# One product split into three one-pass products, and one scan per sequence instead of one per pair

## The chip, the cores and the metric

The kernel runs on one core of one Trainium2 chip. The metric is device time in microseconds, from start to end of one execution. Three runs of the kernel before gave 936.23, 934.80 and 934.54 us, median 934.8 us. The profiled execution took 936.22 us.

## What is computed

The reference is a stack of two layers, each with an attention-like part and a feed-forward part, on x of shape (16, 256, 128), every part followed by a layer norm and a residual. Four parts follow one another:

- L0 attention: a long complex convolution along the sequence. With phazor = r·exp(i·theta) per channel the kernel computes it as a linear recurrence, y[t] = r·y[t-1] + u[t], on the cosine and the sine part of x, and then multiplies back.
- L0 FFN: eight small experts, two picked per token, and a shared expert.
- L1 attention: 16 heads, null keys, ALiBi, causal.
- L1 FFN: four experts, two picked per token. The second one (named `me` in the kernel) is

```
eq  = x @ me_eq_w + me_eq_b
sym = (eq @ me_wv + me_bv) @ me_wo + me_bo
e1  = gelu(sym @ me_c1w + me_c1b) @ me_c2w + me_c2b
```

The three linear maps before `me_c1w` and `me_c1w` itself are folded on chip into one 128x256 weight, `w_me`, so that the expert is `gelu(x @ w_me + b_me) @ w_c2`. The "first product" of the second expert is x @ w_me.

## The kernel before

**Tiling.** The 16 sequences are worked on in 8 groups of SEQ = 2 sequences, that is N = 512 tokens as T = 4 tiles of 128. A group passes through four stages, named by the first letter of their steps: `e` (convolution), `l` (L0 FFN), `a` (L1 attention), `f` (L1 FFN). In the steady state one pass of the tables holds `f` of group i-1, `a` of group i, `l` of group i+1 and `e` of group i+2.

**Order.** Nothing is scheduled on the fly. For every engine (PE, DVE, ACT, POOL) there are tables of step names, lines 36 to 185: PROLOGUE, FIRST, MIDDLE (played five times), LAST_L, LAST_A, LAST_F. An engine runs its steps in the order of its table and waits on semaphores inside them. All loads and stores of the steady state are issued by SP.

**Steps that the change and the prediction touch.**

- `s_decay` (L1298 to L1303, DVE, once): fills `decay_row` with r per channel, 512 columns, and sets columns 0 and 256 to zero, so that one scan over 512 columns restarts at the second sequence.
- `e_scan` (L1432 to L1443, DVE, once per group): two products of the transposed input with the cosine and sine tables (L1438), then two scans of 512 columns (L1443). Both scan operands lie in SBUF. The tensor_tensor_scan is `state = decay*state + u`.
- `s_gain2` (L1308, DVE, first group only) and `conv_gains` (L921, POOL): multiply the scans' outputs by the filter. In all groups `conv_gains` waits for the count of `l_conv`.
- `s_fold3` (L1836 on PE, L1104 on ACT): the folded weight is written to PSUM bank 2 and copied to `w_me`. `s_split` (L1372 to L1375, DVE) waits for that copy and signals `all_set`.
- `f_me.0` and `f_me.1` (L2133 to L2143 on PE, L1224 on ACT): for each half of the 256 hidden rows one fp32 matmul with 128 rows of weights and 512 columns, on `xm_full`, the float32 copy of the transposed, normalised tokens. ACT takes the gelu of each.
- `mm3` (L1761 to L1765, PE): a product of split operands. Every operand is kept as `hi`, rounded to fp32r, and `lo`, the rest, also fp32r. Three fp32r matmuls accumulate hi·hi, hi·lo and lo·hi. It is what `f_sw`, `f_ml`, `a_m`, `a_k`, `a_v`, `l_g` and `l_u` already use. The split tokens `xm` of the L1 FFN are made by ACT (`xm.hi`, L1212) and by DVE (`xm.lo`, `f_lows`, L1645, which counts `f_low`).
- `mask` (L944 to L959, POOL): for each attention unit two selects in place (L949) and one sum of two SBUF tensors (L959). DVE's `e_scan` stands between `a_mix.1` and `a_mix.2` in MIDDLE and POOL's selects run beside it.

In MIDDLE `f_me.0` follows `f_sw.0`, and `f_me.1` follows `f_ce2` and precedes `a_v.0`. In LAST_L it is `f_me.0` after `a_k.2`, `f_me.1` between `f_ml.1` and `f_ml.2`; in LAST_A `f_me.0` after `f_sw.1`, `f_me.1` after `f_sw.2`. In LAST_F, the last group alone, `f_me.0 f_me.1` come right after `f_ce.1` and before `f_sw.0`.

Of the kernel before, what the change touches and what calls it, by code (L numbers as in the profile page):

```python
# [18 lines left out]
F32 = mybir.dt.float32  # L19
# [3 lines left out]
ALU = mybir.AluOpType  # L23
ACT = mybir.ActivationFunctionType
AX_X = mybir.AxisListType.X

P = 128
# [201 lines left out]
def program(nc, a, out):  # L229
    x = a["L0_attn_x"]  # L230
    B, L, D = x.shape
    SEQ = 2
    G = B // SEQ
    T = SEQ * L // P
    N = T * P
# [9 lines left out]
    start = 2.0 ** (-2.0 ** (-1.0))  # L245
# [7 lines left out]
    with ExitStack() as ctx:  # L253
        def sb(name, shape, dt=F32):
            return ctx.enter_context(nc.sbuf_tensor(name, shape, dt))

        def sem(name):
            return ctx.enter_context(nc.semaphore(name))

        def signal(name, per):  # L260
            return Signal(sem(name), per)

        bank = [ctx.enter_context(nc.psum_tensor(f"bank{i}", [P, 512], F32)) for i in range(8)]
# [10 lines left out]
        def split_weight(name, width):  # L274
            return Split(sb(name + "_hi", [P, width], F32R)[:], sb(name + "_lo", [P, width], F32R)[:])
# [14 lines left out]
        conv_a = sb("conv_a", [P, L])  # L290
        conv_b = sb("conv_b", [P, L])
        conv_c = sb("conv_c", [P, L])
        decay_row = sb("decay_row", [P, N])
        vec = sb("vec", [P, 40])
        slope = sb("slope", [P, H])
        bias_k0 = sb("bias_k0", [P, H])
# [17 lines left out]
        w_sw1 = split_weight("w_sw1", I1)  # L314
        w_sw3 = split_weight("w_sw3", I1)
        w_sw2 = sb("w_sw2", [P, J1, P])
        w_me = sb("w_me", [P, 2 * P])
        w_c2 = sb("w_c2", [P, 2, P])
        w_f1 = sb("w_f1", [P, 2 * P])
        w_f2 = sb("w_f2", [P, 2, P])  # L320
# [22 lines left out]
        xm = xlT  # L343
        conv = sb("conv", [P, 4, N])
# [74 lines left out]
        col = {n: vec[:, i:i + 1] for i, n in enumerate(vlist)}  # L419
# [27 lines left out]
        time = kT[:, 0, 0:L + 1]  # L447
# [46 lines left out]
        f_scaled = sem("f_scaled")  # L494
        f_rounded = sem("f_rounded")
        f_split = sem("f_split")
        colb_made = sem("colb_made")
        nk_summed = sem("nk_summed")
        nk_rooted = sem("nk_rooted")
# [32 lines left out]
        def use(kind, t=0, k=0):  # L532

            return ring.index((kind, t, k))
# [3 lines left out]
        l_conv = signal("l_conv", 6)  # L538
# [49 lines left out]
        f_low = signal("f_low", 2)  # L588
# [6 lines left out]
        f_me = signal("f_me", 2)  # L595
# [49 lines left out]
        def ending(g):  # L645
            return g == G - 1
# [4 lines left out]
        def me_bank(g, j):  # L651
            return bank[2 + j] if ending(g) else bank[7]
# [13 lines left out]
        def xm_full(g):  # L666
            return xin[:].rearrange("p t d -> p (t d)") if ending(g) else conv[:, 2, :]
# [16 lines left out]
        def half(h):  # L684
            return slice(2 * h * P, 2 * h * P + 2 * P)
# [36 lines left out]
        def first(g):  # L722
            return known(g) and g == 0
# [272 lines left out]
        def _(act):  # L996
            n = [0]

            def made_by(i):
                n[0] += 1  # L1000
                i.then_inc(act_made, 1)
# [99 lines left out]

            def s_fold3():
                act.wait_ge(pe_made, 8)
                made_by(act.activation(w_me[:], bank[2][:, 0:256], ACT.Copy))  # L1104
                assert n[0] == ACT_MADE

            def to_cols(g):
# [148 lines left out]
        def _(dve):  # L1256
            n = [0]

            def link(i):

                n[0] += 1
                i.then_inc(made, 1)
                dve.wait_ge(made, n[0])
# [5 lines left out]
            V = nc.vector  # L1269
# [28 lines left out]
            def s_decay():  # L1298
                dve.wait_ge(act_made, 2)
                dve.wait_ge(pool_made, POOL_TIME)  # L1300
                dr = decay_row[:].rearrange("p (s t) -> p s t", s=SEQ)
                link(V.tensor_scalar(dr, time[:, 0:L].unsqueeze(1).to_broadcast([P, SEQ, L]), 0.0, col["r"], ALU.mult, ALU.add))
                link(V.memset(dr[:, :, 0:1], 0.0))  # L1303

            def s_gain2():
                dve.wait_ge(conv_set, 2)
# [64 lines left out]

            def s_split():  # L1372
                dve.wait_ge(act_made, ACT_MADE)
                dve.wait_ge(alibi_made, 11)
                dve.sem_inc(all_set, 1)  # L1375

# [55 lines left out]
            def e_scan(g):  # L1432

                if first(g):
                    dve.wait_ge(act_made, 5)
                dve.wait_ge(l_turned.sem, l_turned.at(g, 1))
                for k, w in enumerate((cos_t, sin_t)):
                    V.tensor_tensor(conv[:, k, :].rearrange("p (s t) -> p s t", s=SEQ),  # L1438
                                    bank[7][:].rearrange("p (s t) -> p s t", s=SEQ),
                                    w[:, 0:L].unsqueeze(1).to_broadcast([P, SEQ, L]), ALU.mult).then_inc(l_conv.sem, 1)  # L1440
                for k in range(2):
                    dve.wait_ge(l_conv.sem, l_conv.at(g, 1 + k))
                    V.tensor_tensor_scan(conv[:, 2 + k, :], decay_row[:], conv[:, k, :], 0.0, ALU.mult, ALU.add).then_inc(l_conv.sem, 1)  # L1443

            def e_sum(g):
                dve.wait_ge(l_gain.sem, l_gain.at(g))
# [311 lines left out]
        def _(pe):  # L1758
            mm = nc.tensor.matmul

            def mm3(dst, left, right):  # L1761

                mm(dst, left.hi, right.hi, start=True, stop=False)  # L1763
                mm(dst, left.hi, right.lo, start=False, stop=False)  # L1764
                return mm(dst, left.lo, right.hi, start=False, stop=True)  # L1765
# [188 lines left out]
            def free(g, n):  # L1954
                if n >= 3:
                    pe.wait_ge(a_took.sem, a_took.at(g, n - 2))

            def a_m(g, t):
                for k in range(2):
                    n = use("m", t, k)  # L1960
                    free(g, n)
                    if k == 0:
                        pe.wait_ge(l_low.sem, l_low.at(g, 3 + t // 2))
                    if first(g) and t == 0 and k == 0:
                        pe.wait_ge(kv_split, 1)
                        pe.wait_ge(q_split, 1)
                    mm3(bank[n % 3][:], xaT[:, t * P:(t + 1) * P], w_q[:, 512 * k:512 * k + 512]).then_inc(a_put.sem, 1)

            def a_k(g, i):
# [163 lines left out]
            def f_me_(g, j):  # L2133
                js = slice(j * P, (j + 1) * P)
                if ending(g):
                    pe.wait_ge(f_cols.sem, f_cols.at(g))
                elif j:
                    pe.wait_ge(f_meg.sem, f_meg.at(g, 1))
                    pe.wait_ge(f_relu.sem, f_relu.at(g, 2))
                else:  # L2140
                    pe.wait_ge(f_pick.sem, f_pick.at(g, 2))
                    pe.wait_ge(f_ced.sem, f_ced.at(g, 2))
                mm(me_bank(g, j)[:], w_me[:, js], xm_full(g), start=True, stop=True).then_inc(f_me.sem, 1)  # L2143

            def f_ml_(g, j):
                js = slice(j * P, (j + 1) * P)
# [75 lines left out]
def build(nc, inputs):  # L2222

    arrays, args = {}, {}
    for name, value in inputs.items():
        v = np.ascontiguousarray(value)
        arrays[f"in_{name}"] = v
        args[name] = nc.dram_tensor(f"in_{name}", v.shape, mybir.dt.from_np(v.dtype), kind="ExternalInput").ap()
    out = nc.dram_tensor("out_0", inputs["L0_attn_x"].shape, F32, kind="ExternalOutput").ap()
    program(nc, args, out)  # L2230
    return arrays
# [10 lines left out]
```

## Time and profile before

| what | value |
|---|---|
| median of three runs | 934.8 us |
| profiled execution: time of the run | 936.22 us |
| profiled execution: span of the trace | 934.5 us |
| PE busy | 878.2 us, 94% of the span |
| DVE busy | 754.7 us, 81% |
| ACT busy | 589.0 us, 63% |
| POOL busy | 559.8 us, 60% |
| chain that ended last | PE 68%, DVE 19%, ACT 5%, POOL 4%, issue 3% |
| mean granted TensorE clock | 0.992 |

The time of a run is longer than the trace's span by what lies around the first and the last instruction, here 1.7 us. A matmul's record is longer than the distance to the next one, since matmuls overlap; costs of matmuls are read from the distance of starts. An fp32 matmul leaves two records.

### The profile page before, as it was taken

To read this page: it belongs to the slowest core of one execution; us is meant where nothing else is said; L and a number is where in the kernel's file an instruction comes from. 1 tells how busy PE (TensorE), PEld (TensorE's weight loads), DVE (VectorE), ACT (ScalarE), POOL (GpSimd) and SP (SyncE) were. 2 spreads that over 40 slices of the span, in tenths; PEclk is the share of its full clock that TensorE was granted. 3 is DMA by queue.
4 is the path that set the end of the run, shared out by engine and by line. 5 is a ranking of instruction groups with operands and counts; after the bars stand their busy time and mean duration, and the time that the engine had idled before them with its cause. 6 is when DMAs were issued, how large, how long until landed. Compare 5 with 4: busy or idle time off the path is not lost.

```text
span 934.5 us, 21349 instructions
## 1 busy us (share of the span) xinstructions
PE 878.2 (94%) x8095; PEld 697.0 (75%) x8095; DVE 754.7 (81%) x2457; ACT 589.0 (63%) x1255; POOL 559.8 (60%) x503
## 2 busy tenths in 40 slices
PE   1798899999999999999999999999999999999886
PEld 0585678688777878688787878688787878677666
DVE  6894798779887898879897898879988688955476
ACT  4428773966658672976648673885738673786621
POOL 5235764677546864667636864568646954558523
PEclk9999999999999999999999999999999999999999
DMA  6400000000000000000000000000000000000000
GB/s 162 114 1 0 13 2 2 1 13 2 14 1 1 12 2 13 1 13 1 14 1 1 13 2 14 1 12 2 10 5 1 1 2 14 0 1 1 14 1 12
DMA packets 21992, 11.46 MB, mean 12 GB/s; under 512 B 7553, under 2 KB 21249, under 8 KB 21761
## 3 DMA queue, kind: packets, MB, share of 16 engines
q1 hardware_dynamic: 20032, 9.50, 3.8%
q8 instruction: 64, 1.05, 0.5%
q10 hardware_dynamic: 1856, 0.59, 0.3%
q14 instruction: 40, 0.32, 0.1%
HBM read 7.99 MB, written 2.10 MB: 11 GB/s over the span
## 4 chain that ended last, share of the span: by engine, by line
PE 68%; DVE 19%; ACT 5%; POOL 4%; issue 3%; DMA 0%; DVEq 0%; ACTq 0%; POOLq 0%
PE bank L1763 8%; PE bank L1764 6%; PE bank L1765 6%; PE bank L1776 5%; PE bank L2020 5%; PE bank L2077 4%; PE bank L1929 4%; PE bank L2194 3%; PE bank L2092 3%; PE bank L2200 3%; PE bank L2026 3%; PE bank L2079 2%; PE bank L2067 2%; PE bank L2196 2%; PE bank L2176 2%
## 5 line engine op out<-in xcount | busy, mean ns | idle before, releaser
L935 POOL TENSOR_TENSOR rnorm<-sumsq,minus_half 128x16 f32<-128x16 f32 x32 | 95.6, 2996 | 64.2 <-DVE sumsq L1566 64.2
L2020 PE MATMUL bank<-qT,kT 64*128 64x256 f32 x512 | 96.3, 387 | 0.0
L941 POOL TENSOR_TENSOR rnorm<-unit,minus_half 128x16 f32<-128x16 f32 x32 | 93.1, 2921 | 2.2 <-DVE unit L1572 2.2
L1199 ACT ACTIVATE square<-bank,bias_k,rnorm 128x256 f32<-128x256 f32 x128 | 65.7, 571 | 40.9 <-PE bank L2020 40.9
L2026 PE MATMUL bank<-qT,kT 64*128 64x128 f32 x512 | 84.1, 284 | 5.1 <-ACT unit L1205 3.3
L2026 PEld LDWEIGHTS bank<-qT,kT 64*128 64x128 f32 x512 | 71.0, 186 | 18.7 <-issue 5.7
L1129 ACT ACTIVATE xaT_hi<-bank 128x256 fp32r<-128x256 f32 x16 | 5.9, 384 | 111.9 <-PE bank L1937 111.6
L949 POOL TENSOR_SCALAR_AFFINE_SELECT square<-square 128x512 f32<-128x512 f32 x64 | 46.5, 730 | 48.0 <-ACT square L1205 48.0
L2020 PEld LDWEIGHTS bank<-qT,kT 64*128 64x128 f32 x512 | 68.9, 186 | 0.3
L949 POOL TENSOR_SCALAR_AFFINE_SELECT unit<-unit 128x512 f32<-128x512 f32 x64 | 40.6, 639 | 45.3 <-ACT unit L1205 45.2
L2092 PE MATMUL bank<-w_out,qT 128*128 128x128 f32 x512 | 62.8, 276 | 1.2 <-DVE qT L1615 1.2
L2092 PEld LDWEIGHTS bank<-w_out,qT 128*128 128x128 f32 x512 | 59.7, 192 | 2.1 <-DVE qT L1615 1.5
L1199 ACT ACTIVATE unit<-bank,bias_k,rnorm 128x256 f32<-128x256 f32 x96 | 51.4, 573 | 15.1 <-PE bank L2020 15.1
L1205 ACT ACTIVATE unit<-bank,bias_k,rnorm 128x128 f32<-128x128 f32 x128 | 52.7, 478 | 0.0
L1205 ACT ACTIVATE square<-bank,bias_k,rnorm 128x128 f32<-128x128 f32 x128 | 52.4, 473 | 0.0
L1580 DVE TENSOR_TENSOR unit<-unit,rnorm 128x1024 f32<-128x1024 f32 x32 | 40.9, 1280 | 10.0 <-POOL rnorm L935 10.0
L1172 ACT ACTIVATE val<-bank 128x512 f32<-128x512 f32 x64 | 37.3, 604 | 17.5 <-PE bank L1765 15.3
L1776 PEld LDWEIGHTS bank<-ident,unit 128*128 128x128 f32 x296 | 34.1, 142 | 18.7 <-DVE unit L1580 9.3
L1138 ACT ACTIVATE unit<-bank 128x512 f32<-128x512 f32 x64 | 37.3, 598 | 15.1 <-PE bank L1765 13.5
L1776 PE MATMUL bank<-ident,unit 128*128 128x128 f32 x296 | 40.5, 278 | 6.6 <-DVE unit L1580 3.5
L1615 DVE TENSOR_TENSOR qT<-bank,mixed 128x512 f32<-128x512 f32 x64 | 44.2, 691 | 2.2
L1563 DVE TENSOR_REDUCE sumsq<-square 128x16 f32<-128x1024 f32 x32 | 38.9, 1215 | 8.0 <-ACT square L1145 8.0
(419 smaller groups left out, 2900.8 us busy)
## 6 DMA issues: line engine op xcount, KB each, us to landing
xin<-in_L_attn_x SPq DMA_DIRECT2D x7, 256.0 KB, 2.7
out<-x SPq DMA_DIRECT2D x7, 256.0 KB, 2.3
square<-in_L_attn_w_kv SPq DMA_DIRECT2D x1, 1024.0 KB, 6.5
unit<-in_L_attn_w_q SPq DMA_DIRECT2D x1, 512.0 KB, 5.2
w_out<-in_L_attn_w_out SPq DMA_DIRECT2D x8, 64.0 KB, 2.1
xin<-in_L_attn_x ACTq DMA_DIRECT2D x1, 256.0 KB, 3.2
unit<-in_L_ffn_experts_gate ACTq DMA_DIRECT2D x1, 256.0 KB, 3.4
unit<-in_L_ffn_experts_up SPq DMA_DIRECT2D x1, 256.0 KB, 2.8
```

The costliest lines, as they stand in the source:

```text
L935: pool.tensor_tensor(rnorm[:, 1, t, :], sumsq[:, t % 2, :], minus_half[:], ALU.pow).then_inc(a_root.sem, 1)
L941: pool.tensor_tensor(rnorm[:, 0, ts, hs], k_sumsq[:, ts, hs], minus_half[:, hs].unsqueeze(1).to_broadcast([P, 2, H // 2]), ALU.pow).then_i ...
L949: pool.affine_select(out=pd, in_=pd, compare_op=ALU.is_ge, fill=0.0, base=0, pattern=[[0, 4], [1, P]], channel_multiplier=-1).then_inc(a_m ...
L1199: last = act.activation(early(pr, j), k0, ACT.Exp, bias=bias_k0[:, h:h + 1], scale=by)
L1205: last = act.activation(late(pr, j), bank[2][:, 2 * P * s + P * j:2 * P * s + P * (j + 1)], ACT.Exp, bias=bias_k1[:, h:h + 1], scale=by)
L1763: mm(dst, left.hi, right.hi, start=True, stop=False)
L1764: mm(dst, left.hi, right.lo, start=False, stop=False)
L1765: return mm(dst, left.lo, right.hi, start=False, stop=True)
L1776: last = nc.tensor.transpose(dst[:, t * P:(t + 1) * P], src(t), ident[:])
L2020: return mm(bank[s][:, 2 * P * i:2 * P * (i + 1)], kT[rs, p, 2 * P * b:2 * P * b + P], qT[rs, p, 2 * P * b:2 * P * (b + 1)], start=True, s ...
L2026: return mm(bank[2][:, 2 * P * s + P * i:2 * P * s + P * (i + 1)], kT[rs, p, ts], qT[rs, p, ts], start=True, stop=True)
L2092: mm(out_bank(g, h)[:, ts], outT[:, c, ts], w_out[:, c, :], start=(c == 0), stop=False)
```

## The change

The second expert's first product is made by `mm3` on `xm`, so `w_me` becomes a split weight with a `lo` part that DVE makes once in `s_split`, and PE waits for it (`me_split`) before its first use of bank 2. `f_me.0` waits for `f_low`. `decay_row` has half its columns, and each scan of 512 columns becomes two of 256, one per sequence; the semaphore is counted by the last of the two. `xm_full` stays, since `f_ce` reads it.

```diff
-        decay_row = sb("decay_row", [P, N])
+        decay_row = sb("decay_row", [P, L])
...
-        w_me = sb("w_me", [P, 2 * P])
+        w_me = split_weight("w_me", 2 * P)
...
+        me_split = sem("me_split")
...
             def s_fold3():
                 act.wait_ge(pe_made, 8)
-                made_by(act.activation(w_me[:], bank[2][:, 0:256], ACT.Copy))
+                made_by(act.activation(w_me.hi, bank[2][:, 0:256], ACT.Copy))
...
             def s_decay():
-                dr = decay_row[:].rearrange("p (s t) -> p s t", s=SEQ)
-                link(V.tensor_scalar(dr, time[:, 0:L].unsqueeze(1).to_broadcast([P, SEQ, L]), 0.0, col["r"], ALU.mult, ALU.add))
-                link(V.memset(dr[:, :, 0:1], 0.0))
+                link(V.tensor_scalar(decay_row[:], time[:, 0:L], 0.0, col["r"], ALU.mult, ALU.add))
+                link(V.memset(decay_row[:, 0:1], 0.0))
...
             def s_split():
                 dve.wait_ge(act_made, ACT_MADE)
+                V.tensor_tensor(w_me.lo, bank[2][:, 0:2 * P], w_me.hi.bitcast(F32), ALU.subtract).then_inc(me_split, 1)
                 dve.wait_ge(alibi_made, 11)
                 dve.sem_inc(all_set, 1)
...
                 for k in range(2):
                     dve.wait_ge(l_conv.sem, l_conv.at(g, 1 + k))
-                    V.tensor_tensor_scan(conv[:, 2 + k, :], decay_row[:], conv[:, k, :], 0.0, ALU.mult, ALU.add).then_inc(l_conv.sem, 1)
+                    for q in range(SEQ):
+                        last = V.tensor_tensor_scan(conv[:, 2 + k, half(q)], decay_row[:], conv[:, k, half(q)], 0.0, ALU.mult, ALU.add)
+                    last.then_inc(l_conv.sem, 1)
...
                         pe.wait_ge(kv_split, 1)
                         pe.wait_ge(q_split, 1)
+                        pe.wait_ge(me_split, 1)
...
-                mm(me_bank(g, j)[:], w_me[:, js], xm_full(g), start=True, stop=True).then_inc(f_me.sem, 1)
+                if j == 0:
+                    pe.wait_ge(f_low.sem, f_low.at(g))
+                mm3(me_bank(g, j)[:], w_me[:, js], xm).then_inc(f_me.sem, 1)
```

## Rows read from the trace of the kernel before

**Rows 1.** Busy time by stage, two passes of MIDDLE (window, us, engines' busy us).
```profile
383.73:490.05 106.32, 105.58 (x996) 84.55 (x995) 91.11 (x302) 70.71 (x151) 68.28 (x56) 1.00 0.02 7
490.05:597.08 107.03, 105.78 (x996) 84.33 (x995) 92.03 (x302) 70.83 (x151) 67.41 (x57) 1.00 0.02 6
```
**Rows 2.** Records of L2143 outside the last group (ns min/median/max, first and last start).
```profile
L2143 PE MATMUL bank<-conv,w_me x28: 590/592/595, 170.3 to 820.7; 128*128 128x512 f32 x28
```
**Rows 3.** Chain that ended last, its pieces on L2143 (start us, us, what).
```profile
190.42 0.86 PE bank L2143 x2
...
902.14 1.72 PE bank L2143 x4
```
**Rows 4.** Timeline of PE, two split products after a wait (start us, us).
```profile
283.40 0.50 PE L1763 MATMUL bank<-xlT_hi,w_sw_hi 128*128 128x512 f32 x1 [0.21 <-DVE mixed L1705]
...
283.74 0.39 PE L1764 MATMUL bank<-xlT_lo,w_sw_hi 128*128 128x512 f32 x1
...
284.68 0.40 PE L1765 MATMUL bank<-xlT_hi,w_sw_lo 128*128 128x512 f32 x1
```
**Rows 5.** Timeline of PE's weight loads, soon after f_me.0 in a pass of MIDDLE.
```profile
278.61 0.86 PEld L1776 LDWEIGHTS bank<-ident,unit 128*128 128x128 f32 x8 [0.90 <-DVE unit L1580]
```
**Rows 6.** Timeline of the last group around its two products.
```profile
901.66 0.42 DVE L1645 TENSOR_TENSOR xlT_lo<-bank,xlT_hi 128x256 fp32r<-128x256 f32 x1 [1.22 <-ACT xlT_hi L1212]
...
901.97 1.88 PE L2143 MATMUL bank<-xin,w_me 128*128 128x512 f32 x4
```
**Rows 7.** Timeline of DVE in the prologue, scans of the second group with POOL idle.
```profile
53.41 2.33 DVE L1443 TENSOR_TENSOR_SCAN conv<-decay_row,conv 128x512 f32<-128x512 f32 x2
```
**Rows 8.** Single scans of L1443 (ns min/median/max, start us).
```profile
L1443 DVE TENSOR_TENSOR_SCAN conv<-decay_row,conv x1: 1194/1194/1194, 229.4 to 229.4; 128x512 f32<-128x512 f32 x1
...
L1443 DVE TENSOR_TENSOR_SCAN conv<-decay_row,conv x1: 1679/1679/1679, 546.9 to 546.9; 128x512 f32<-128x512 f32 x1
...
L1443 DVE TENSOR_TENSOR_SCAN conv<-decay_row,conv x1: 1662/1662/1662, 548.5 to 548.5; 128x512 f32<-128x512 f32 x1
```
**Rows 9.** Groups of instructions by form, DVE's 512-wide subtraction (busy us, mean ns).
```profile
L1469 DVE TENSOR_TENSOR xlT_lo<-bank,xlT_hi 128x512 fp32r<-128x512 f32 x8 | 5.5, 692 | 16.7 <-ACT xlT_hi L1109 16.7
```
**Rows 10.** Timeline of POOL and DVE around the scans of an ordinary pass of MIDDLE.
```profile
227.11 1.28 POOL L959 TENSOR_TENSOR mixed<-unit 128x512 f32<-128x512 f32 x1
...
228.10 2.48 DVE L1443 TENSOR_TENSOR_SCAN conv<-decay_row,conv 128x512 f32<-128x512 f32 x2
...
229.59 1.42 POOL L949 TENSOR_SCALAR_AFFINE_SELECT square<-square 128x512 f32<-128x512 f32 x1 [1.20 <-ACT square L1205]
```
**Rows 11.** Timeline of POOL around the scans of the fourth pass of MIDDLE.
```profile
546.22 1.27 POOL L959 TENSOR_TENSOR mixed<-unit 128x512 f32<-128x512 f32 x1
...
548.45 0.64 POOL L949 TENSOR_SCALAR_AFFINE_SELECT square<-square 128x512 f32<-128x512 f32 x1 [0.95 <-ACT square L1205]
```
**Rows 12.** A POOL select beside four DVE instructions in a row (timeline, then two of L1391).
```profile
782.03 0.76 POOL L949 TENSOR_SCALAR_AFFINE_SELECT square<-square 128x512 f32<-128x512 f32 x1 [0.97 <-ACT square L1205]
...
L1391 DVE TENSOR_SCALAR x4m<-x4m,n_f_mv,n_f_rstd x1: 341/341/341, 782.0 to 782.0; 128x128 f32<-128x128 f32 x1
...
L1391 DVE TENSOR_SCALAR x4m<-x4m,n_f_mv,n_f_rstd x1: 657/657/657, 782.2 to 782.2; 128x128 f32<-128x128 f32 x1
```
**Rows 13.** Timeline of POOL during the scans in FIRST.
```profile
125.16 1.00 POOL L949 TENSOR_SCALAR_AFFINE_SELECT square<-square 128x512 f32<-128x512 f32 x1 [1.62 <-ACT square L1205]
```
**Rows 14.** Timeline of the prologue, scans of the first group.
```profile
14.03 2.67 DVE L1443 TENSOR_TENSOR_SCAN conv<-decay_row,conv 128x512 f32<-128x512 f32 x2
...
15.73 2.03 POOL L921 TENSOR_TENSOR conv<-conv,conv_a 128x512 f32<-128x512 f32 x1 [1.22 <-DVE conv L1443]
...
16.81 1.50 DVE L1308 TENSOR_TENSOR conv<-conv,conv_b 128x512 f32<-128x512 f32 x1
```
**Rows 15.** Timeline of DVE late in the prologue, the step that PE's l_x.0 waits for.
```profile
62.89 0.60 DVE L1413 TENSOR_SCALAR ce_rows<-x2n,n_a_mv,n_a_rstd 128x128 f32<-128x128 f32 x2
```
**Rows 16.** Chain that ended last, PE late in the prologue.
```profile
63.39 2.23 PE bank L1789 x5
```

## Prediction

> **What bounds the kernel now.** I read the windows by stage first. In an ordinary pass of MIDDLE PE is busy 105.58 of 106.32 us [rows 1]: it has under 1 us to spare, and the other engines matter where they make it wait. The chain of waits, read next, says where: 68% of it is PE, 19% DVE. Two stretches of a pass concern this change. Early on the chain runs through DVE and POOL (the norms of the third expert), later `f_me.1` is on PE's own part of it. Around `e_scan` chain and engines are nearly level, and one pair of windows tells how level: in the fourth pass the two scans took 0.78 us more than in an ordinary one (below), and that pass is 0.71 us longer than the one before it [rows 1]. So at that place DVE has almost no slack, by this estimate 0.07 us.
>
> **Part 1, the product.** One fp32 product leaves two records of 592 ns [rows 2] but takes 0.86 us of the chain [rows 3], 0.43 per record, since matmuls overlap. A split product starts its matmuls 0.235 us apart (four steps from 283.74 to 284.68 [rows 4]), so it takes 0.70; its first one after a wait adds 0.11 for the weights (0.34 between the first two starts [rows 4]), which an fp32 one would need too. Each product saves 0.16 us of PE, 16 of them (14 of [rows 2] and two in the last group) 2.5 us. Which are on the path: the chain holds L2143 once in each of the five passes of MIDDLE (`f_me.1`), twice in LAST_L and twice in LAST_A, nine pieces like the first of [rows 3]: 9 x 0.16 = 1.4 us. The five `f_me.0` of MIDDLE I cost at nothing: soon behind them PE's loads wait 0.90 us for DVE [rows 5], and that wait grows by what the product saves. In the last group the two products are on the chain, 1.72 us [rows 3], but PE now waits for `f_low`: DVE writes `xm.lo` until 902.08 [rows 6], and a first matmul starts about 0.15 later, at 902.23, where it now starts at 901.97 [rows 6]. Six matmuls take 1.40: 0.32 less 0.26 leaves 0.06 us. Nothing but ACT's gelu hangs on it. In the other groups an `f_sw` ahead has waited for `f_low` already: no cost. Sum of part 1: 1.5 us less. Ends: 0.7 (the passes of MIDDLE are held by DVE and only the last three groups count) and 2.5 (all of it).
>
> **Part 2, the scans as instructions.** With POOL idle the pair is recorded with 2.33 us [rows 7], an undisturbed scan with 1.19 [rows 8], so the second starts 1.13 us after the first. The fixed share: DVE's subtraction takes 692 ns for 512 columns [rows 9] and 0.42 us for 256 [rows 6], so 0.15 of a record is fixed, of which 0.06 to 0.09 lies under the next one; I take 0.07 between starts. A scan of 256 columns then starts its successor after 0.60 us and is recorded with about 0.66. Four take 0.14 us more than two. The Trainium skill has a rule against this part, VectorE: DVE Perf Modes, "The DRAIN you can't avoid": the next instruction does not start before the pipe is empty. By it and that page's 150 fixed cycles (0.16 us, its estimate) six groups would lose 1.0 us more than by my sum. The trace does not agree, since the second scan starts before the record of the first ends (2 x 1.19 is more than 2.33).
>
> **Part 2, who gets the memory port.** This is the larger term. In an ordinary pass POOL's select arrives 1.49 us after the scans began, inside the second scan, and is recorded with 1.42 [rows 10] instead of 0.64 us [rows 11]: it was held until the scan ended. In the fourth pass the scans began 0.68 instead of 0.99 us after POOL's L959 and so waited longer for its end; then the select arrived just ahead of the second scan and ran in 0.64 [rows 11], and the scans took 1.68 and 1.66 [rows 8], the pair 3.26 instead of 2.48 [rows 10]. One engine is shut out for a whole instruction of the other. The Trainium skill, SBUF — State Buffer, "SBUF: two separate sides", calls it an exclusive lock between GpSimd and a VectorE instruction with two SBUF inputs; the trace agrees. Who goes first when POOL waits and DVE's next instruction is ready, the trace shows too: the select of 782.03 arrived inside one of four DVE instructions in a row, waited 0.12 and ran, and the DVE instruction issued next took 657 instead of 341 ns [rows 12]. So POOL gets in at a boundary. There was one boundary, now there are three. From the start of the scans: the first is held by L959 for 0.15 (2.48 against 2.33), boundaries lie at 0.75, 1.35 and 1.95; the select arrives at 1.49 in the third scan, gets the port as that ends (about 1.82), is through at 2.46, and the fourth scan, free 0.1 before that, ends at 3.01 instead of 2.48: 0.53 us. Ends: 0.14 (POOL not let in) and 0.85. The slack takes 0.07: 0.46 per pass, 1.8 us for four. The fourth pass has had its collision and pays 0.1.
>
> FIRST: the select is held there for 0.36 us (1.00 against 0.64 [rows 13]), so it will arrive near the third boundary, and DVE loses up to 0.6; the chain runs over ACT and POOL there, and I take 0.15. Prologue, first group: POOL's L921 is held by the second scan and then holds DVE's L1308 to 1.50 us [rows 14]. Afterwards L921 gets in ahead of the fourth scan, that waits, and L1308 follows free: it ends at about 18.7 instead of 18.31, 0.4 us on the chain. `s_decay` gets shorter, but DVE waits for PE behind it: nothing. The subtraction for `w_me.lo` costs 0.42 us like [rows 6], with the longer scans 0.6 us of DVE at 56 us; DVE then ends the input of `l_x.0` at 64.1 instead of 63.5 [rows 15], under PE's warm-up, which lasts to 65.6 [rows 16]: nothing; were that cover gone, 0.4. PE's wait for `me_split` ends 10 us before PE comes to it, and what is queued behind it waits for nothing new. No DMA is moved. Part 2: 1.8 + 0.1 + 0.15 + 0.4 = 2.5 us more.
>
> **Sum.** 936.22 - 1.5 + 2.5 = 937.2 for the profiled execution, which is 1.4 us above the median of 934.8 (half of it may be the collision of its fourth pass). The same change on the median gives 935.8 us.
>
> **Rivals.** Times are on the median; a measurement of this kernel can tell about 0.2% (1.9 us) from no change.
> A, the forecast: 935.8, its own range 934.8 to 936.9.
> B: POOL is not let in between scans, which run back to back. Six groups pay 0.14 and the prologue 0.1, 0.9 less 1.5: 934.2. For it: in ordinary passes the select is held by a running scan. Against: [rows 12].
> C, faster: PE is the bound nearly everywhere, the scans' delay falls into its idle 0.7 us of a pass, and a select that ends up to 0.8 us earlier lets the next unit start sooner. All 2.5 us are gained: 932.3. Against: in the fourth pass the select was as early, and 0.71 us were lost.
> D, slower: the fourth scan waits as long as in the fourth pass, 0.78 us, in each of five passes, and since DVE then leads, they keep nothing of `f_me.1`: 5 x 0.71 + 0.6 in FIRST + 0.4 in the prologue, less 0.7 from the last groups, 3.9 us: 938.7. It decides once the select starts right at the fourth scan's own start instead of 0.15 us before it.
>
> **How the numbers follow.** A 0.42, B 0.20, C 0.18, D 0.20. Faster by over 0.2% (under 932.9): C and a little of B, 0.19. Slower (over 936.7): D and a tenth of A, 0.25. Within: 0.56. The range goes from C to just under D, 932.4 to 938.4.
>
> **What would show it.** Three pieces of 0.23 at nine places of the chain, 0.16 shorter each, and six in the last group from 902.2 on (as far as the rest stays). Four scans per group of 0.66 us, but one of about 1.05 in each pass of MIDDLE, with POOL's select beside it at 0.9 to 1.0 instead of 1.42. Passes of 106.6 us. The forecast is wrong if all scans are 0.66 (B), or if passes stay at 106.3 with a prolonged scan: then DVE had more slack than the fourth pass says. Passes under 106.1 mean C, passes of 107.0 D.

## The result and the profile after

The changed kernel took 938.11 us (median of 7 runs, 937.88 to 939.73), the kernel before 936.07 us in the same session (median of 7, 934.54 to 936.28). The ratio is 1.0028, 95% interval 1.0018 to 1.0037: slower by 1.7 to 3.5 us. That is inside the forecast range, but on the side to which I gave 0.25; "no change" had 0.56. The median of three runs from which I started, 934.8, was itself low: 83 later runs of the kernel before have their median at 936.0.

From the page of the changed kernel, first the busy time of the engines, then the chain that ended last by engine:

```profile
PE 878.3 (94%) x8111; PEld 702.1 (75%) x8111; DVE 757.9 (81%) x2474; ACT 588.2 (63%) x1255; POOL 555.5 (59%) x503
...
PE 57%; DVE 29%; ACT 6%; POOL 4%; issue 3%; DMA 0%; DVEq 0%; SPq 0%; ACTq 0%; POOLq 0%
```

Busy times hardly move (DVE 3 us up, POOL 4 down). The chain does: PE's part falls from 68% to 57%, DVE's rises from 19% to 29%. At many places where PE ended last before, DVE now does.

**Where the time arose.** Every pass reads the router's logits once (DVE, the first of the two instructions that write `logit` from `bank,b_router`). The distances of these instructions cut the trace into an opening, seven stretches and an end, here for the profiled run of each kernel (us):

| kernel | opening | 1 | 2 | 3 | 4 | 5 | 6 | 7 | 1 to 7 | end |
|---|---|---|---|---|---|---|---|---|---|---|
| before | 167.46 | 106.27 | 106.23 | 106.32 | 107.03 | 113.45 | 105.49 | 91.93 | 736.72 | 30.3 |
| before, second trace | 166.46 | 106.20 | 106.20 | 106.32 | 106.96 | 113.41 | 105.48 | 91.89 | 736.46 | 30.3 |
| after | 169.36 | 106.74 | 107.17 | 106.82 | 107.01 | 113.88 | 105.37 | 91.70 | 738.69 | 30.0 |
| after, second trace | 167.98 | 106.72 | 107.15 | 106.81 | 107.01 | 114.04 | 105.33 | 91.73 | 738.79 | 29.9 |

Stretches 1 to 5 hold the five `e_scan` of MIDDLE. The stretches repeat within 0.1 us from trace to trace (0.16 once), which the run times do not: so a few tenths in a stretch can be read, and the scatter sits in the opening. The sum of seven repeats less well, to 0.26 us for the kernel before. In stretches 1 to 7 the change costs 2.0 us between the first traces, 2.3 between the second.

**The scans.** Timeline of the changed kernel, first and last scan of the ordinary pass that answers to [rows 10], with POOL's select; then the first and third scan of the fourth pass and POOL's select there:

```profile
229.85 0.87 DVE L1445 TENSOR_TENSOR_SCAN conv<-decay_row,conv 128x256 f32<-128x256 f32 x1
...
231.80 1.05 DVE L1445 TENSOR_TENSOR_SCAN conv<-decay_row,conv 128x256 f32<-128x256 f32 x1
...
231.34 0.97 POOL L950 TENSOR_SCALAR_AFFINE_SELECT square<-square 128x512 f32<-128x512 f32 x1 [1.17 <-ACT square L1206]
...
550.66 1.14 DVE L1445 TENSOR_TENSOR_SCAN conv<-decay_row,conv 128x256 f32<-128x256 f32 x1
...
552.31 1.08 DVE L1445 TENSOR_TENSOR_SCAN conv<-decay_row,conv 128x256 f32<-128x256 f32 x1
...
552.21 0.63 POOL L950 TENSOR_SCALAR_AFFINE_SELECT square<-square 128x512 f32<-128x512 f32 x1 [0.96 <-ACT square L1206]
```

This is what the forecast named: one scan of 1.05 us, POOL's select at 0.97 instead of 1.42, the four scans 3.00 us instead of 2.48 for the two. POOL gets the port at the boundary between two scans and the next scan waits.

**The product.** The changed kernel's mm3 on `w_me` in the last group, timeline of PE:

```profile
906.10 0.47 PE L1766 MATMUL bank<-xlT_hi,w_me_hi 128*128 128x512 f32 x1
...
906.88 0.40 PE L1766 MATMUL bank<-xlT_hi,w_me_hi 128*128 128x512 f32 x1
...
907.58 0.40 PE L1766 MATMUL bank<-xlT_hi,w_sw_hi 128*128 128x512 f32 x1
907.82 0.40 PE L1767 MATMUL bank<-xlT_lo,w_sw_hi 128*128 128x512 f32 x1
```

Three matmuls take 0.70 us, as reckoned. But stretches 1 and 3 are 0.5 us longer, where the scans alone were to give 0.46 and the product to give back 0.16. Something of the forecast's 1.5 us is missing, and that was the question for the experiments. Where an experiment below has one trace, its stretches are set against the first trace of the kernel before, and a difference of 0.3 us in a sum of seven is within what that kernel's own two traces show.

### The profile page after: what moved, and what is told of

Its sections match the earlier page's. It is cut to its first block, busy times and chain, and to the rows that moved or that the text cites. A ratio compares the mean times of both kernels' runs of the same rounds, so it can differ in the third digit from the quotient of the medians.

```text
span 938.0 us, 21400 instructions
## 1 busy us (share of the span) xinstructions
PE 878.3 (94%) x8111; PEld 702.1 (75%) x8111; DVE 757.9 (81%) x2474; ACT 588.2 (63%) x1255; POOL 555.5 (59%) x503
## 3 DMA queue, kind: packets, MB, share of 16 engines
q8 instruction: 64, 1.05, 0.5%
## 4 chain that ended last, share of the span: by engine, by line
PE 57%; DVE 29%; ACT 6%; POOL 4%; issue 3%; DMA 0%; DVEq 0%; SPq 0%; ACTq 0%; POOLq 0%
PE bank L1766 7%; PE bank L1768 6%; PE bank L1767 6%; PE bank L1779 4%; PE bank L2081 4%; PE bank L1932 3%; PE bank L2024 3%; DVE x4m L1718 3%; PE bank L2096 2%; DVE conv L1445 2%; PE bank L2083 2%; PE bank L2030 2%; PE bank L2200 2%; PE bank L2206 2%; PE bank L2071 2%
## 5 line engine op out<-in xcount | busy, mean ns | idle before, releaser
L950 POOL TENSOR_SCALAR_AFFINE_SELECT square<-square 128x512 f32<-128x512 f32 x64 | 44.2, 695 | 51.7 <-ACT square L1206 51.7
L1583 DVE TENSOR_TENSOR unit<-unit,rnorm 128x1024 f32<-128x1024 f32 x32 | 41.0, 1280 | 10.2 <-POOL rnorm L936 10.0
```

The source lines that it names most:

```text
L950: pool.affine_select(out=pd, in_=pd, compare_op=ALU.is_ge, fill=0.0, base=0, pattern=[[0, 4], [1, P]], channel_multiplier=-1).then_inc(a_m ...
```

## The experiments

Theory 1: the scans cost what I gave them or a little more, and the product gained nothing in the passes of MIDDLE. Theory 2: the product gained its 1.5 us and the scans cost 3.5 to 4.

### One part at a time

`e1_product`: the changed kernel's product, the scans of before. The low part of the weights is borrowed from another weight, and the subtraction that makes it is left out, so the product's lowest bits are wrong.

```diff
-        w_me = sb("w_me", [P, 2 * P])
+        w_me_hi = sb("w_me_hi", [P, 2 * P], F32R)[:]
...
+        w_me = Split(w_me_hi, w_ml1.lo[:, 0:2 * P])
...
-                mm(me_bank(g, j)[:], w_me[:, js], xm_full(g), start=True, stop=True).then_inc(f_me.sem, 1)
+                if j == 0:
+                    pe.wait_ge(f_low.sem, f_low.at(g))
+                mm3(me_bank(g, j)[:], w_me[:, js], xm).then_inc(f_me.sem, 1)
```

> The product part alone: f_me as three one-pass products of split tokens and weights, the scans as before (two of 512 columns, row of decays of full length). The low part of the weights is read from the first 256 columns of w_ml1's low part instead of a tensor of its own, so the subtraction that makes it is left out and f_me's lowest bits are wrong. By the steps of the prediction: 1.5 us faster than the kernel before (ratio 0.9984), scans unchanged at 2.33 to 2.48 us a pair. Rival, that the nine products on the chain are paid back by a wait elsewhere in the pass: within 0.4 us of before (0.9996 to 1.0004). Rival, that PE's wait for f_low, which now stands ahead of f_me.0, costs something in every pass: slower by 0.5 us or more.

`e2_scans`: the kernel before with `decay_row` of half the length, as in the change, and

```diff
-                    V.tensor_tensor_scan(conv[:, 2 + k, :], decay_row[:], conv[:, k, :], 0.0, ALU.mult, ALU.add).then_inc(l_conv.sem, 1)
+                    for q in range(SEQ):
+                        last = V.tensor_tensor_scan(conv[:, 2 + k, half(q)], decay_row[:], conv[:, k, half(q)], 0.0, ALU.mult, ALU.add)
+                    last.then_inc(l_conv.sem, 1)
```

> The convolution part alone: four scans of 256 columns with the half-long row of decays, the product as before (one fp32 matmul). By the steps of the prediction: 2.5 us slower than the kernel before (ratio 1.0027). If the product's gain is real (1.5 us) and the scans cost more than I gave them, 3.5 to 4.5 us slower (1.0037 to 1.0048). If the changed kernel lost because the product gained nothing: 2.0 to 2.8 us slower here, and the product alone within 0.4 us of before.

Measured, with the stretches as above:

| kernel | median us (runs) | ratio to before | 1 | 2 | 3 | 4 | 5 | 6 | 7 | 1 to 7 |
|---|---|---|---|---|---|---|---|---|---|---|
| e1_product | 935.14 (11) | 0.9990 [0.9982, 0.9999] | 106.24 | 106.22 | 106.24 | 107.01 | 113.46 | 105.33 | 91.74 | 736.24 |
| e2_scans | 938.04 (11) | 1.0018 [1.0009, 1.0027] | 106.87 | 106.95 | 106.88 | 107.03 | 114.20 | 105.49 | 91.88 | 739.29 |

In stretches 1 to 7 the product gains 0.48 us and the scans cost 2.57, together 2.09; the changed kernel shows 1.97. Against the second trace of the kernel before they are 0.22 and 2.83. The two parts add up, and theory 2 falls. The product gains 0.16 and 0.19 in stretches 6 and 7 (about half of the 0.32 that I gave to each of them for its two pieces) and next to nothing in 1 to 5: 0.03, 0.01, 0.08, 0.02 and none. The scans cost 0.60, 0.72, 0.56, 0 and 0.75: nothing in the fourth pass, which had its collision already, and more than my 0.46 in the others.

### What costs in the scans: a boundary at the wrong moment

`e3_first_pair` and `e4_second_pair` split only one of the two scans of a group, `if k == 0` or `if k == 1` around the loop of `e2_scans`; the other stays one scan of 512.

> The kernel before with only the first of the two scans of a group split in two of 256, the second in one of 512 columns. If what costs is the boundary between two scans at which POOL's waiting select gets in, it makes nothing here, because the select comes while the scan of 512 runs: only the overhead of an instruction, 0.07 us a group, 0.3 to 0.6 us in all (1.0003 to 1.0006). If each extra scan costs by itself, whatever POOL does: half of what the scans alone cost, 1.2 to 2 us (1.0013 to 1.0021).

> The kernel before with only the second of the two scans split in two of 256, the first in one of 512 columns. If the boundary lets POOL's select in: the last scan of a pass of the middle of the kernel takes 1.05 us instead of 0.66 and POOL's select 0.97 instead of 1.42, about 2.0 us slower in all (1.0021). If each extra scan costs by itself: the same as with the first scan split, 1.2 to 2 us, and the last scan takes 0.66.

| kernel | median us (runs) | ratio to before | 1 | 2 | 3 | 4 | 5 | 6 | 7 | 1 to 7 |
|---|---|---|---|---|---|---|---|---|---|---|
| e3_first_pair | 934.37 (11) | 0.9986 [0.9977, 0.9995] | 106.28 | 106.27 | 106.27 | 106.96 | 113.47 | 105.48 | 91.85 | 736.58 |
| e4_second_pair | 937.74 (12) | 1.0018 [1.0010, 1.0027] | 106.88 | 106.87 | 106.87 | 107.02 | 114.09 | 105.46 | 91.85 | 739.04 |

Both add one instruction per group. Splitting the first scan costs nothing (in stretches 1 to 7 it lies between the two traces of the kernel before, 736.58 against 736.72 and 736.46), splitting the second 2.32 us, 90% of what both splits cost. The median of e3_first_pair is 1.6 us under that of the kernel before; its stretches show none of that, so it lies in the opening and the end (below). The timelines of the same pass, e3_first_pair and then e4_second_pair, scans and POOL's select:

```profile
332.99 1.42 DVE L1445 TENSOR_TENSOR_SCAN conv<-decay_row,conv 128x256 f32<-128x256 f32 x2
334.33 1.19 DVE L1448 TENSOR_TENSOR_SCAN conv<-decay_row,conv 128x512 f32<-128x512 f32 x1
...
334.48 2.24 POOL L949 TENSOR_SCALAR_AFFINE_SELECT square<-square 128x512 f32<-128x512 f32 x2 [1.20 <-ACT square L1205]
```

```profile
334.92 1.37 DVE L1448 TENSOR_TENSOR_SCAN conv<-decay_row,conv 128x512 f32<-128x512 f32 x1
336.22 1.63 DVE L1445 TENSOR_TENSOR_SCAN conv<-decay_row,conv 128x256 f32<-128x256 f32 x2
...
336.41 0.90 POOL L949 TENSOR_SCALAR_AFFINE_SELECT square<-square 128x512 f32<-128x512 f32 x1 [1.20 <-ACT square L1205]
```

In both the select arrives 1.49 us after the scans began. In the first it finds a scan of 512 columns that has just begun and has to wait for its end; DVE loses nothing. In the second it finds a scan of 256, gets in behind it, and the last scan waits for it. (The POOL line of e3_first_pair holds two selects; the first alone takes 1.48 us, the second 0.64 as in the kernel before.) So the count of instructions is innocent (my 0.14 us per group was too high); what costs is a boundary between the arrival of POOL's instruction and the end of DVE's row of scans.

**Why 0.6 and not 0.46.** The scans themselves lose 0.48 us (2.96 against 2.48). The rest comes 6 us behind their end. Timeline of the kernel before, then of e2_scans, DVE's L1620/L1621 and the POOL select next to it, and where DVE stands then. Counted from the start of stretch 2 (273.73 and 274.20 us) DVE comes at 69.15 and at 69.64, POOL at 69.54 and at 69.56:

```profile
342.88 0.22 DVE L1620 TENSOR_TENSOR mixed<-mixed,recip 128x64 f32<-128x64 f32 x1
...
343.27 0.64 POOL L949 TENSOR_SCALAR_AFFINE_SELECT unit<-unit 128x512 f32<-128x512 f32 x1 [0.76 <-ACT unit L1205]
```

```profile
343.76 0.64 POOL L949 TENSOR_SCALAR_AFFINE_SELECT unit<-unit 128x512 f32<-128x512 f32 x1 [0.78 <-ACT unit L1205]
...
343.84 0.64 DVE L1621 TENSOR_TENSOR mixed<-mixed,recip 128x64 f32<-128x64 f32 x1
...
347.79 0.47 DVE L1602 STREAM_TRANSPOSE bank<-bank 128x256 f32<-128x256 f32 x1 [0.34 <-PE bank L2071]
```

DVE, now 0.49 us late, comes to a small product of two SBUF tensors just after the next select instead of just before it, and takes 0.64 us for 0.22 us of work. Part of that is made up (DVE's sum at L1449, 344.91 us, meets POOL's L959 in the kernel before and takes 0.90 us; here, at 346.05, it comes behind it and takes 0.68), part reaches PE, on which DVE waits 0.34 us at 347.79, a wait that the kernel before lacks. I had costed the first collision and not asked what a DVE that is half a microsecond late would meet next.

### Where the product's gain went

In `e1_product` PE runs 0.16 us ahead of the kernel before from `f_me.1` on, for 27 us, and is level again at the second gate product of the next group (the first, at 321.70 and 319.94 us, still comes ahead). These are the places in the kernel before, then in e1_product: POOL's bias product, DVE's variance step beside it, and that gate product of PE; at the end the two last pieces of e1_product's chain. Stretch 2 starts at 273.73 and 272.12 us, so the gate product comes 51.07 us into it in both.

```profile
313.65 1.05 POOL L980 TENSOR_TENSOR x<-row_out,pick 128x512 f32<-128x512 f32 x1
...
314.13 0.59 DVE L1386 TENSOR_SCALAR n_x_var<-n_x_mv 128x4 f32<-128x4 f32 x1
...
324.80 0.51 PE L1763 MATMUL bank<-xlT_hi,w_gate_hi 128*128 128x512 f32 x1
```

```profile
312.03 1.05 POOL L982 TENSOR_TENSOR x<-row_out,pick 128x512 f32<-128x512 f32 x1
...
312.36 0.74 DVE L1389 TENSOR_SCALAR n_x_var<-n_x_mv 128x4 f32<-128x4 f32 x1
...
323.19 0.50 PE L1766 MATMUL bank<-xlT_hi,w_gate_hi 128*128 128x512 f32 x1
...
322.54 0.60 DVE unit L1524
...
323.19 0.50 PE bank L1766
```

An instruction on 128x4 elements takes 0.17 us when it is undisturbed. Here it starts beside a running POOL product and ends with it, at 314.70 in the kernel before (313.65 + 1.05). In e1_product the step comes 0.16 us earlier in the pass and takes 0.15 longer: 0.74 instead of 0.59. POOL's products have not moved (39.92 and 39.91 us into the stretch). From that step on DVE works without a gap over 0.11 us (router, coefficients, sixteen mixing steps, `unit`) up to 323.1, and PE's gate product waits for it. In the kernel before `unit` ends at 324.75 and the gate product starts at 324.80: DVE and PE arrive there together. So the gain seems to end at a collision on the port again. Two ways to test it: move DVE's step, or take POOL's product away.

**Moving DVE's step.** First, a version that needs no borrowed weights: `e5_both_wide` is the changed kernel with its true `w_me.lo` and the two wide scans.

```diff
-        self.six = sb(name + "_six", [P, 4, 6])
+        self.six = SIX[0]
...
-        decay_row = sb("decay_row", [P, L])
+        decay_row = sb("decay_row", [P, N])
```

> The changed kernel with its true split weights, but the scans as before: two of 512 columns with a row of decays of full length. The kilobyte this needs comes from letting all norms share one scratch tile for their statistics (written and read by VectorE alone, in order). If the changed kernel's loss lies in the scans alone: like the product alone, 0.9 us faster than before (ratio 0.9990), no scan split, a pass of the middle the same 106.24 us as before. If the subtraction that makes the low part of the weights, or its wait, costs as much as a scan: 0.3 to 0.6 us less gain.

`e6_var_later` is the kernel before, and `e7_both_var` is e5_both_wide, each with this edit of MIDDLE's DVE table (`e_six` is `e_stats` without its last instruction, the variance step, and `e_var` is that instruction):

```diff
-l_turn3 e_stats l_route l_pick l_coef a_nT
+l_turn3 e_six l_route l_pick l_coef e_var a_nT
```

> The kernel before with one VectorE instruction of a pass moved: n_x's variance step (L1386) goes from ahead of the router's logits to behind the coefficients, away from the POOL product that it waits for now (0.59 us instead of 0.17). Nothing is left out. If TensorE alone bounds that stretch: no change (0.9996 to 1.0004), passes of 106.2. If VectorE bounds it: 0.4 us a pass faster, 2 us in all (0.9978).

> e5_both_wide with that same step of VectorE moved. If what swallows the product's 0.16 us a pass is VectorE's wait for POOL at that step (TensorE and VectorE arrive together at the first gate product after it): the passes of the middle come to 106.1, 0.16 us each below e5_both_wide where the move alone brings nothing, 1.5 us faster than before in all (0.9984). If something else takes the gain: passes of 106.24, the same time as e5_both_wide. If the move only shifts the wait for POOL to another instruction: slower than e5_both_wide by some tenths.

| kernel | median us (runs) | ratio to before | 1 | 2 | 3 | 4 | 5 | 6 | 7 | 1 to 7 |
|---|---|---|---|---|---|---|---|---|---|---|
| e5_both_wide | 934.50 (12) | 0.9991 [0.9982, 1.0000] | 106.22 | 106.23 | 106.18 | 106.98 | 113.43 | 105.34 | 91.75 | 736.13 |
| e6_var_later | 936.48 (12) | 1.0010 [1.0000, 1.0020] | 106.26 | 106.28 | 106.38 | 107.05 | 113.51 | 105.48 | 91.88 | 736.84 |
| e7_both_var | 935.48 (12) | 0.9997 [0.9987, 1.0007] | 106.25 | 106.25 | 106.24 | 107.00 | 113.46 | 105.31 | 91.68 | 736.19 |

`e5_both_wide` repeats the product alone (736.13 against 736.24): the subtraction and PE's wait for it cost nothing that shows in the stretches. The move brings nothing in either kernel, and the timeline of e7_both_var says why: DVE's router subtraction, POOL's sum beside it, and the variance step in its new place:

```profile
315.27 0.94 DVE L1516 TENSOR_TENSOR exp<-top 128x32 f32<-128x32 f32 x1
...
314.89 1.27 POOL L989 TENSOR_TENSOR ce_rows<-ce_rows,x 128x512 f32<-128x512 f32 x1
...
317.63 0.16 DVE L1387 TENSOR_SCALAR n_x_var<-n_x_mv 128x4 f32<-128x4 f32 x1
```

The variance step is down to 0.16 us, and the next small instruction with two SBUF inputs, 0.24 us before, takes 0.94 until POOL's following sum has ended (314.89 + 1.27 = 316.16). The wait moved, which was my third case, though the time stayed the same instead of getting worse. (MAX8 and FIND_INDEX8 ahead of it ran as long beside POOL as without it in e8_both_pool_less, four MAX8 in 0.37 us.)

**Taking POOL's product away.** In `e9_pool_less` (from the kernel before) and `e8_both_pool_less` (from e5_both_wide) the last product and sum of `f_bias` are left out for all groups but the last, so the fourth expert's bias is missing from the output:

```diff
+                    if e == E1 - 1 and not ending(g):
+                        for _ in range(2):
+                            pool.sem_inc(f_bias.sem, 1)
+                        continue
```

> The kernel before without the last two POOL instructions of f_bias (the fourth expert's bias product and its sum, 1.05 + 1.27 us a group; that bias is missing in the output of all groups but the last). POOL then no longer holds the port when VectorE comes to n_x's variance (0.59 us) or to the router's subtraction (0.24 us). If POOL sets the pace of that stretch together with TensorE: passes of the middle 106.1 to 106.25, no more than 0.1 us below before, because TensorE is the bound at once. If VectorE's wait for POOL is all that bounds it: 0.4 us a pass faster.

> e5_both_wide (split product, wide scans) without the same two POOL instructions. If the product's 0.16 us a pass was swallowed by VectorE's wait for POOL there, it comes out now: passes of the middle 0.16 us shorter than those of e9_pool_less, about 106.05. If it is swallowed by something else: the same passes as e9_pool_less to 0.03 us.

| kernel | median us (runs) | ratio to before | 1 | 2 | 3 | 4 | 5 | 6 | 7 | 1 to 7 |
|---|---|---|---|---|---|---|---|---|---|---|
| e9_pool_less | 935.20 (10) | 0.9994 [0.9985, 1.0004] | 106.18 | 106.23 | 106.33 | 107.00 | 113.42 | 105.41 | 91.91 | 736.48 |
| e8_both_pool_less | 934.83 (10) | 0.9990 [0.9980, 0.9999] | 106.11 | 106.06 | 106.09 | 106.83 | 113.29 | 105.12 | 91.72 | 735.22 |

With POOL out of the way DVE's step takes 0.17 us in both (315.65 in e8_both_pool_less):

```profile
315.65 0.17 DVE L1396 TENSOR_SCALAR n_x_var<-n_x_mv 128x4 f32<-128x4 f32 x1
...
326.30 0.51 PE L1773 MATMUL bank<-xlT_hi,w_gate_hi 128*128 128x512 f32 x1
```

The second line is the gate product, 50.88 us into its stretch (which starts at 275.42) instead of 51.07: the 0.16 us are kept at the very place where they were lost.

For the kernel before that is worth next to nothing, because PE is level with DVE there (0.24 us in seven stretches). But now the product shows: 0.07, 0.17, 0.24, 0.17 and 0.13 in stretches 1 to 5, 0.29 and 0.19 in the last two, 1.26 in all against 0.48 to 0.59 with POOL's instructions in place. That is nearly the 1.4 us that the nine pieces on the chain promised. This settles where the gain of MIDDLE went: the product is 0.16 us cheaper, and DVE, held by POOL's `f_bias`, reached the gate product as late as PE did. The run times are too coarse to show it (medians 0.4 us apart).

### The opening and two fixed gaps

> The changed kernel once more, for a second trace. From the router's logits of the third group on it should repeat the first trace's passes to 0.05 us (106.74, 107.17, 106.82, 107.01). If the 1.9 us that it lost ahead of 167 us in the first trace is the clock that TensorE was granted in the opening, the milestone comes up to 2 us earlier or later here with the granted clock of the stretches 30 to 110 us; if it belongs to the change, it repeats.

> The kernel before once more, for a second trace: passes of 106.27, 106.23, 106.32 and 107.03 us to within 0.05, and the third group's logits anywhere within 1.7 us of the first trace's 167.46 us if the opening's time is a matter of the granted clock.

Their stretches are in the first table. The opening came out at 167.98 and 166.46 us, 1.4 and 1.0 us below the first traces, with the same instructions. The windows of 30 to 60 us, of the kernel before and then of the changed one (columns as in [rows 1]: behind the busy times the granted clock, then DMA share and GB/s):

```profile
30.00:60.00 30.00, 25.95 (x166) 19.02 (x165) 26.51 (x77) 10.30 (x36) 6.21 (x9) 1.00 0.28 69
```

```profile
30.00:60.00 30.00, 26.50 (x151) 18.97 (x151) 25.25 (x74) 10.04 (x36) 3.94 (x6) 0.94 0.26 69
```

and inside them split products of PE in the changed kernel:

```profile
38.91 0.63 PE L1767 MATMUL bank<-xlT_lo,w_gate_hi 128*128 128x512 f32 x1
39.33 0.63 PE L1768 MATMUL bank<-xlT_hi,w_gate_lo 128*128 128x512 f32 x1
```

Their starts are 0.42 us apart; in the kernel before they are 0.23 apart there, as everywhere later. TensorE stood at the lower of its two levels, 1.2 instead of 2.4 GHz, from the sixth of eight small router products on, which follow an idle time of 1.05 us. In the first trace of the kernel before the same idle time and products were followed by the full level, in its second by the lower one:

```profile
38.00:47.00 9.00, 8.87 (x24) 5.59 (x24) 6.42 (x29) 2.18 (x5) 0.00 (x0) 0.50 0.57 157
```

Such spells fall in different places from program to program and from run to run up to about 110 us; from there to 925 us the granted clock is 1.00 in these traces. In all TensorE stood at the lower level for 13.7 us of the opening in both traces of the changed kernel, for 10.2 and 13.7 us in the two of the kernel before. A run's opening can be had from its span less what follows the opening in that kernel's trace: 83 runs of the kernel before give 165.5 to 169.5 us, mean 167.0; the parts alone give means of 166.9 (e1_product), 166.8 (e2_scans), 166.3 (e3_first_pair) and 166.7 (e5_both_wide), the changed kernel's seven runs 168.1. So the changed kernel's opening came out some 1.0 us longer, though none of its parts shows that by itself. That need not be work of the change: e7_both_var and e8_both_pool_less do in the opening just what e5_both_wide does, since their edits begin with the third group's pass, and yet their means are 167.7 (12 runs) and 168.1 (10 runs) against 166.7 (12). Of my terms for the opening one is seen: in the first group the fourth scan waits for L922, and L1308 follows undisturbed:

```profile
14.05 3.66 DVE L1445 TENSOR_TENSOR_SCAN conv<-decay_row,conv 128x256 f32<-128x256 f32 x4
17.81 0.69 DVE L1308 TENSOR_TENSOR conv<-conv,conv_b 128x512 f32<-128x512 f32 x1
```

It ends at 18.50 us, 0.2 later than before, not 0.4. In FIRST no scan is held by a select: the four take 2.54 us instead of 2.44 for the two. How the rest comes about, whether by where the slow spells fall or by 0.2 us here and 0.3 us of subtraction there, stays open; no run took a single term of the opening by itself.

Two more tenths-sized items belong to no theory. In the end of the kernel before DVE stands 0.46 us between two instructions of the last group, with nothing to wait for but its own previous one; the changed kernel has 0.11 us there (end 30.0 instead of 30.3) but has a gap of the same size in stretch 2, in both of its traces. First the kernel before, then the changed one:

```profile
927.18 1.12 DVE L1722 SCALAR_TENSOR_TENSOR x<-bank,pick,x 128x128 f32<-128x128 f32 x4 [0.46 <-DVE x L1715]
```

```profile
368.26 0.42 DVE L1420 TENSOR_TENSOR x2n<-xn,x 128x256 f32<-128x256 f32 x1 [0.46 <-DVE xn L1414]
```

The first is there in the second trace of before, in e6_var_later and in e9_pool_less too, and missing in e2_scans and e4_second_pair (scans alone) as in e1_product and e5_both_wide (product alone). It goes with the program and not with what the change computes. Why was not tried.

## Why the prediction was wrong

By its own steps, in the order of the text:

- **A split product takes 0.70 instead of 0.86 us:** right ([rows 3] against 0.70 from start to start), and 0.16 us per pass appears in full once POOL is out of the way.
- **Nine pieces on the chain are worth 9 x 0.16 = 1.4 us:** wrong, and this is the step that failed. It is worth 0.48 us (0.22 by the second trace of the kernel before): nothing to speak of in the five passes of MIDDLE, half of the 0.32 in each of the next two. The chain names the path that ended last, not the lead it has over the second. DVE's wait at L1386, 0.42 us of a 0.59 us instruction, was in the trace of before at 314.13 us, and with it the runner-up was level with PE (324.75 against 324.80). e9_pool_less and e8_both_pool_less show it: with that wait gone the product gains 1.26. For LAST_L and LAST_A no trace was followed to the place where the other half goes. My lower end for part 1, 0.7 us, named this very case ("held by DVE and only the last three groups count"), and I took 1.5.
- **The five `f_me.0` of MIDDLE are worth nothing:** right. e1_product is level again within two microseconds.
- **The last group gains 0.06 us:** it gains nothing. From DVE's `xm.lo` to the second matmul of `f_sw`, which follows on the two products, it takes 2.29 us (905.53 to 907.82), before 2.27 (901.66 [rows 6] to 903.93).
- **An extra instruction costs 0.07 us between starts:** too much. e3_first_pair adds one per group and loses nothing in the stretches. Undisturbed scans of 256 start 0.58 us after one another, two of 512 1.13 [rows 7, 8]. By the rule of the Trainium skill that I set against my sum (VectorE: DVE Perf Modes, "The DRAIN you can't avoid") six groups would have lost 1.0 us more than by it; the trace does not agree, since the extra instruction costs less than my sum, not more. I had read the rule too widely: the same section says that a next instruction that is not held starts earlier, and with that the starts 0.58 us apart, under a record of 0.66, agree.
- **POOL gets in at the third boundary, the fourth scan waits:** right in mechanism, place and size, 1.05 us and 0.97 us as forecast, 0.48 to 0.52 us longer scans per pass against 0.53.
- **The slack takes 0.07 of it:** wrong sign, and the second term that was mis-sized. A pass loses 0.6 us (0.75 in the fifth), since the delayed DVE runs into POOL's next select at L1620. Four passes 2.6 us instead of 1.8. The fourth pass pays 0 instead of 0.1.
- **FIRST 0.15, prologue 0.4, subtraction nothing:** 0.2 of the 0.4 is seen in the first group, and in FIRST the collision did not come at all. The opening as a whole came out about 1.0 us longer in the mean, by as much as it also differs between programs that do the same in it.

The sum for the profiled execution was 937.2: 1.5 off and 2.5 on. Measured in its terms: 0.5 off, 2.6 on in the stretches (the two parts together 2.0 in the changed kernel), 1.0 on in the opening, 0.35 off in the end, together 2.6 us instead of 1.0. The ratio gives 2.6, the session's means lie 2.7 apart and its medians 2.0. Of the 2.6 only the 2.0 of the stretches have a shown cause. Of the 2.3 us between 938.1 and the forecast's 935.8, 1.3 are the base of 934.8, which was low, and 1.0 are the change; my reason for its distance from the profiled run, the collision of the fourth pass, was wrong too, since both traces of the kernel before have that pass at 107.0. Rival D had the right sign and both halves of the cause (nothing kept of `f_me.1`, and more than 0.46 us per pass), and for f_me.1 the right reason, that DVE leads. Its price per pass was too high (0.71 against 0.6, and the fourth pass pays nothing), its 0.6 us in FIRST did not come, and that its 938.7 is so near is luck in part: the low base and the unexplained opening filled the gap. I gave it 0.20 because I read DVE's near-zero slack at the scans and did not carry it over to the product.

## What to carry to other kernels

When the profile shows DVE and POOL both near the path and both at work on SBUF, a DVE instruction cut in two is a door for POOL: look when POOL's next instruction arrives. A cut before that costs nothing, a cut behind it costs what POOL's instruction has left, once more wherever the late DVE meets POOL again. And before a saving on the chain is counted, look for the runner-up: short DVE instructions that take several times their usual length are places where another engine may already set the pace, and here the move of such an instruction only handed the wait to the next one.

`e5_both_wide` keeps the cheaper product and the wide scans and computes all that the changed kernel does. It is 2.6 us faster than the changed kernel in stretches 1 to 7 and, at 0.9991 [0.9982, 1.0000], at best 0.2% faster than the kernel before, a difference that this measurement hardly tells from none.

## What I had not expected of the hardware

VectorE instructions of a few elements wait for the shared port as long as the big ones: 128x4 elements took 0.59 to 0.74 us beside a POOL product instead of 0.17, 128x32 took 0.94 instead of 0.17 (its time in e8_both_pool_less), 128x64 took 0.64 instead of 0.22. POOL's power function did not do that: beside it (316.12 us on, in e7_both_var) the small instructions of the router kept their 0.16 to 0.29 us. And a VectorE that waits for no other engine can stand about 0.35 us longer than usual (0.46 against 0.11) at a place that was the same in both traces of a program and changed with an edit elsewhere: of two kernels that differ by a few tenths, the gap may be all of it.
